# A graph layer kernel: query weights folded into the first mix weight, keys centred in their weights, one-hot rows built by ScalarE in fp32r, longer rings, and a fourth accumulator

## The reference

```
gathered = edge_vals[:, None] * xn[dst]
new_x    = segment_sum(gathered, src)            # graph branch
out1     = tanh(batchnorm(new_x @ hamilton1));   gnn = out1 @ hamilton2

q, k, v  = split(xn @ w_qkv + b_qkv)             # mix branch, 8 heads of 32
k, v     = ln(k), ln(v)                          # per head, with gain and offset
kv       = k^T v / N                             # per head, 32 x 32
ret      = q @ kv + xn
mix      = gelu(ret @ w1 + b1) @ w2 + b2 + xn

x        = x + gnn + mix
x        = x + top2_of_8_experts(layernorm(x))
```

## Time and profile before

| what | value |
|---|---|
| median of three runs | 2387.26 us |
| the profiled execution's own time | 2384.72 us |
| its span, first to last instruction | 2383.3 us |
| busy share of the span: TensorE, VectorE, ScalarE, GpSimd | 81%, 72%, 47%, 54% |
| mean granted TensorE clock | 0.89 of full speed |
| first and last put start | 108.4 and 1352.2 us |
| bytes moved by DMA, mean rate | 401.93 MB, 169 GB/s |

### The profile page before, as it was taken

One profiled execution on the slowest core, in us unless ns is written; L12 is line 12 of the kernel. 1 busy time (PEld: TensorE's weight loads), 2 busy tenths in 40 slices (PEclk: granted clock), 3 DMA queues, 4 the chain that ended last, 5 costly groups with the idle time before them and its releaser, 6 DMA issues. The chain is left out here.

```text
span 2383.3 us, 38273 instructions
## 1 busy us (share of the span) xinstructions
PE 1934.3 (81%) x11227; PEld 1607.3 (67%) x11251; DVE 1713.1 (72%) x5437; ACT 1128.4 (47%) x2236; POOL 1278.8 (54%) x811
## 2 busy tenths in 40 slices
PE   2559997697888878887877266985899999999995
PEld 1437775565665656656666134872799999999995
DVE  4848898687767858673333076888788888988884
ACT  1324443222232332323222114236899999999993
POOL 1447787578778877766777600000355444455542
PEclk8579998799998989888999598665899999999997
DMA  7878877477787787868888673223588888878885
GB/s 232 283 189 153 168 115 126 76 127 121 122 156 132 125 163 134 177 98 192 176 171 165 97 223 112 68 89 107 150 232 233 234 232 233 232 233 234 233 233 167
DMA packets 325710, 401.93 MB, mean 169 GB/s; under 512 B 34841, under 2 KB 267054, under 8 KB 325364
## 3 DMA queue, kind: packets, MB, share of 16 engines
q1 hardware_dynamic: 193822, 256.71, 34.9%
q0 software_dynamic: 103008, 103.83, 32.2%
q10 hardware_dynamic: 28662, 38.84, 5.3%
HBM read 251.12 MB, written 154.55 MB: 170 GB/s over the span
## 5 line engine op out<-in xcount | busy, mean ns | idle before, releaser
L1094 POOL DMA_INDIRECT acc_dram<-third x566 | 914.6, 1616 | 343.0 <-issue 138.6
L2016 POOL DMA_INDIRECT sum_dram<-node,small x112 | 198.2, 1770 | 316.4 <-DVE node L1945 222.7
L1873 PE MATMUL bank<-up_parts 128*128 128x256 f32 x2688 | 334.4, 284 | 2.3 <-DVE up_parts L1903 2.3
L1886 PE MATMUL bank<-down_parts 128*128 128x256 f32 x2688 | 335.4, 284 | 0.0
L1873 PEld LDWEIGHTS bank<-up_parts 128*128 128x128 f32 x2688 | 329.2, 193 | 2.7 <-DVE up_parts L1903 2.7
L1886 PEld LDWEIGHTS bank<-down_parts 128*128 128x128 f32 x2688 | 325.3, 191 | 0.0
L551 PE MATMUL bank<-work,third 128*128 128x256 f32 x1132 | 294.4, 403 | 27.8 <-ACT third L1049 27.7
L1049 ACT ACTIVATE third<-bank 128x512 f32<-128x512 f32 x283 | 168.6, 597 | 290.1 <-DMA acc_dram<-third 234.5
L857 DVE TENSOR_SCALAR third<-fixed,third 128x128 f32<-128x128 f32 x566 | 164.2, 369 | 161.0 <-PE bank L540 142.0
L1998 POOL DMA_INDIRECT node<-xh_dram,small x112 | 135.5, 1209 | 242.2 <-DVE small L1699 208.4
L551 PEld LDWEIGHTS bank<-work,third 128*128 128x128 f32 x1132 | 217.9, 205 | 63.9 <-ACT third L1049 31.6
(11 more groups left out here) (268 smaller groups left out, 3237.4 us busy)
## 6 DMA issues: line engine op xcount, KB each, us to landing
turned<-in_w_up SPq DMA_DIRECT2D x56, 1024.0 KB
turned<-in_w_down SPq DMA_DIRECT2D x56, 1024.0 KB
work<-src_dram SPq DMA_DIRECT2D x141, 256.0 KB
acc_dram<-fixed SPq DMA_DIRECT2D x15, 1280.0 KB, 13.2
work<-xn_dram SPq DMA_DIRECT2D x146, 128.0 KB
work<-acc_dram SPq DMA_DIRECT2D x72, 256.0 KB, 3.5
at_dram<-turned ACTq DMA_DIRECT2D x48, 256.0 KB
work<-at_dram ACTq DMA_DIRECT2D x24, 512.0 KB, 4.5
```

What stands on the lines that cost most here:

```text
L1094: e.indirect_dma_start(acc_dram[i], bass.IndirectOffsetOnAxis(put_i[:, t:t + 1], 0), M[:, t % (2 * QUAD), :], None, compute_op=ALU.add).th ...
L1873: k = e.matmul(ps, W1s[:, 2 * b + wp, q, h * P:(h + 1) * P], xTs[:, 2 * b + xp, q, :], start=(q == 0 and (wp, xp) == TERMS[0]), stop=(q == ...
L1886: k = e.matmul(bank[5 + c][:, 0:D], hTs[:, hp, h, c * P:(c + 1) * P], W2s[:, 2 * b + wp, h, :], start=(h == 0 and hp == 0 and wp == 0), st ...
L2016: e.indirect_dma_start(sum_dram, bass.IndirectOffsetOnAxis(slot_i[:, n:n + 1], 0), yb[:, i % 2, c, :], None, compute_op=ALU.add).then_inc( ...
```

## The change

It does these things:

1. **Folded mix weights.** Since `ret = (xn @ Wq + bq) @ KV + xn`, the product `ret @ w1` equals `xn @ (Wq KV w1 + w1)` plus a constant row. Four new key steps work out `Wq KV w1`, add it to `Wm1`, and the constant to the bias. The query product, its bias, the `KV` product and the addition of `xn` go, for all 13 chunks; 51 mix steps stay of 102.
2. **Centred key weights.** The head mean is subtracted from the columns of `Wkv` and from the bias once, so that keys and values leave TensorE centred. VectorE's sum and subtraction of each of the 49 tiles go. ScalarE squares straight from the PSUM bank, then copies.
3. **Sums beside the keys.** A column of ones stands beside the values, so that one of the two extra columns of sums comes with the 128 columns of the product.
4. **fp32r halves and ScalarE's ones.** Edge weights are split once into a high part and a rest; `one_lo` becomes two fp32r matrices, made by one `scalar_tensor_tensor` of 256 columns; `one_hi` is made on ScalarE as `relu(1 - abs(iota + far))`, two activations of 294 to 344 columns; TensorE does two fp32r matmuls. The first group's width goes from 5 to 6 (245 to 294 columns). One more step of distance lies between making and adding. `A` is set to zero by ScalarE, 512 columns at a time.
5. **Three-quad rings** for `OH` and `M`, and three buffers for the turned `A`.
6. **Four accumulators**, the fourth used from the 25th put on; 20 fills instead of 15; 100 loads instead of 75 in the node stage, and VectorE's first addition there 1024 columns wide instead of 512.
7. **Costs.** New step costs, with which the keys take quads 0 to 44, mix and dense 44 to 113, the products 113 to 137. The index is made by a maximum instead of a product and a sum.

The diff, cut to its core:

```diff
-N_ACC = 3
+N_ACC = 4
-EARLY = (4, 12)
+EARLY = (4, 12, 24)
-DENSE = ((0, 108, 5), (108, 152, 6), (152, 188, 6), (188, 216, 7))
+DENSE = ((0, 108, 6), (108, 152, 6), (152, 188, 6), (188, 216, 7))
+ROW_QUADS = 3
...
-        costs = [2.0] + [2.8] * (NT + 4) + [1.0] * 2 + cost_in_turn + [2.4] * (2 * PRODUCTS)
+        costs = [0.6] * 3 + [0.9] * NT + [0.4] * 4 + [0.5] * 4 + cost_in_turn + [0.53] * (2 * PRODUCTS)
...
         def keys_tensor(e):
-                    for i in range(2):
-                        k = e.matmul(bank[6 + g][:, P + i:P + i + 1], kvn[...i * D + g * P...], ones[0:rows, 0:1], ...)
+                    e.matmul(bank[6 + g][:, 0:P + 1], keys, beside_one, start=(t == 0), stop=False)
+                    k = e.matmul(bank[6 + g][:, P + 1:P + 2], values, ones[0:row.shape[0], 0:1], ...)
...
+            for g in range(2):
+                e.matmul(bank[6 + g][:, 0:D], KV[:, g, :], WqT[:, g, :], start=True, stop=False)
+                e.matmul(bank[6 + g][:, D:D + 1], KV[:, g, :], cols[:, 0, g:g + 1], start=False, stop=True)
+            for m in range(KC):
+                for g in range(2):
+                    k = e.matmul(bank[6 + m][:, 0:D], folded[:, g, m * P:(m + 1) * P], Wm1[:, g, :], ...)
...
         def mix_tensor(e):
-                    for q in range(KC):
-                        k = e.matmul(mix_bank(n)[:, 0:w], Wqkv[:, q, m * P:(m + 1) * P], xnT_ring[...], ...)
-                    e.matmul(mix_bank(n)[:, 0:w], KV[:, m, :], qT[:, m, 0:w], start=True, stop=True)
+                for q in range(KC):
+                    k = e.matmul(bank[5][:, 0:w], Wm1[:, q, m * P:(m + 1) * P], xnT_ring[:, c % 2, q, 0:w], ...)
...
         def dense_tensor(e):
-                for i in range(b - a + 2):
-                    t = a + i - 1
+                for i in range(b - a + 3):
+                    t = a + i - 2
+                        e.wait_ge(s_away, HOT_DONE[t])
-                        e.matmul(dense_bank(n)[:, 0:HI * s], one_lo[:, t % 4, :], one_hi[:, t % 3, 0:HI * s], ...)
+                        for i_ in range(2):
+                            k = e.matmul(dense_bank(n)[:, 0:even(HI * s)], one_lo[:, t % 4, i_, :],
+                                         one_hi[:, t % 3, 0:even(HI * s)], start=(i_ == 0), stop=(i_ == 1))
...
         def keys_vector(e):
+            centre(heads(Wkv[:, 0, :]))
+            centre(heads(Wkv[:, 1, :]))
+            centre(heads(bkv))
-                    e.tensor_reduce(ksum, rows, AX.X, ALU.add)
-                    e.scalar_tensor_tensor(out=d3, in0=spread16(ksum), scalar=-1.0 / HD, in1=rows, ...)
...
         def mix_vector(e):
-                    e.tensor_tensor(ret[:, m, 0:w], mix_bank(n)[:, 0:w], xnT_ring[:, c % 2, m, 0:w], ALU.add)
...
         def dense_vector(e):
-                        e.tensor_scalar(one_lo[:, t % 4, :], iota_p, lo_col[:, t:t + 1], w_c[:, t:t + 1], ...)
-                        e.tensor_scalar(one_hi[:, t % 3, 0:HI * s], iota_n[:, 0:HI * s], hi_col[:, t:t + 1], None, ...)
+                        e.scalar_tensor_tensor(out=one_lo[:, t % 4], in0=iota_p.unsqueeze(1).broadcast_to((P, 2, P)),
+                                               scalar=lo_col[:, t:t + 1], in1=parts_w[:, t, :]..., ...)
-                    e.memset(A, 0.0).then_inc(s_clear, 1)
...
         def keys_scalar(e):
-                    e.activation(kvq, kvn[:, t % 4, :], ACT.Square)
-                    e.activation(kvs[:, i % 2, :], bank[5][:, :], ACT.Copy)
+                    e.activation(kvq, bank[5][:, :], ACT.Square)
+                    e.activation(kvn[:, i % 5, 1:2 * D + 1], bank[5][:, :], ACT.Copy)
...
         def mix_scalar(e):
-                    e.activation(qT[:, m, 0:w], mix_bank(n)[:, 0:w], ACT.Identity, bias=cols[:, 0, m:m + 1])
...
         def dense_scalar(e):
+                        e.activation(away[:, t % 2, 0:even(HI * s)], iota_n[...], ACT.Abs, bias=far_col[:, t:t + 1])
+                        e.activation(one_hi[:, t % 3, 0:even(HI * s)], away[:, t % 2, ...], ACT.Relu, bias=ones[:, 0:1],
+                                     scale=-1.0)
+                            cleared = clear(k)
...
         def scalar_edges(e):
-                    if q >= 2:
-                        for u in (t - 2 * QUAD, t + 1 - 2 * QUAD):
+                    if q >= ROW_QUADS:
+                        for u in (t - ROW_QUADS * QUAD, t + 1 - ROW_QUADS * QUAD):
                             e.wait_ge(s_put[acc_of[u]], 16 * nth_put[u])
...
         def vector_nodes(e):
-                e.tensor_tensor(sums[:, 0, 0:n * D], sums[:, 0, 0:n * D], sums[:, 2, 0:n * D], ALU.add)
+                e.tensor_tensor(sums[:, 0:2, 0:n * D], sums[:, 0:2, 0:n * D], sums[:, 2:4, 0:n * D], ALU.add)
```

More of the change, by code:

```diff
@@ L135, in gps_layer @@
         X = node(NT, D)
+        HOT_WORDS = 4 * 2 * P + 3 * LINE
+        with nc.sbuf_tensor("hots", [P, HOT_WORDS], F32R) as hots:
+            one_lo = hots[:, 0:8 * P].rearrange("p (n a b) -> p n a b", n=4, a=2)
+            one_hi = hots[:, 8 * P:HOT_WORDS].rearrange("p (n a) -> p n a", n=3)
         turned = region("turned", NT * D)
@@ L138, in gps_layer @@
         turned.again()
+        turned(HOT_WORDS)
         A = turned(HI, P)
@@ L163, in gps_layer @@
         third = region("third", NT * D, late)
-        work = region("work", 13064, late)
+        work = region("work", 13060 + NG, late)
         src_c = third(EG * P)
         w_c = third(EG * P)
-        trash_minus = third(EG * P)
         dup = third(EG * P)
@@ L464, in mix_tensor @@
+                    if len(pair_of(c, m)):
+                        for t in pair_of(c, m):
+                            down(t)
                         yield
@@ L587, in keys_vector @@
                 vec.wait()
+                if row is b2row:
+                    for end in (0, 2 * D + 1):
+                        vec.done(e.memset(kvn[:, :, end:end + 1], 1.0))
+                    vec.wait()
                 e.scalar_tensor_tensor(out=row_b, in0=r, scalar=ident[:, 2:3], in1=row_b, op0=ALU.mult, op1=ALU.add).then_inc(s_bias, 1)
@@ L636, in keys_vector @@
                 vec.wait()
-                vec.done(e.tensor_copy(sums, bank[6 + g][:, P:P + 2]))
+                for i, at in enumerate((0 if g == 0 else P, P + 1)):
+                    vec.done(e.tensor_copy(sums[:, i:i + 1], bank[6 + g][:, at:at + 1]))
                 vec.wait()
```

448 lines of the change are left out of this document (231 added, 217 removed).

## The result

The changed kernel takes 2421.5 us (median of 4, 2417.5 to 2439.7) against 2386.1 of the kernel before on the same chip: ratio 1.0165, 95% interval 1.0109 to 1.0220. It is slower, where 2286 and faster was forecast. The profiled execution took 2417.6 us, with a span of 2416.1.

A forecast was written before the change was run, and what follows sets the result against it. GpSimd's puts were taken as the bound: minus 121 us for faster puts, plus 7 for the start, plus 13 for the read-back, minus 101 in sum, gave 2284, with the median's offset 2286 us; range 2248 to 2345.

The forecast's parts named there:

- Each engine falls below the puts' pace: Mix and dense quads: TensorE 6.2, VectorE 5.9, ScalarE 6.0 us against four puts' 7.46, so GpSimd's puts set the pace.
- the 7 us counted for the start: Start of the edge stage: five more fills delay VectorE about 20 us; 7 us taken as loss, bounds 0 and 20.
- TensorE's work: Edge stage, 147 to 1300 us: folding, centring and fp32r products cut TensorE's 964 us by 153, to 811.
- The dense products: TensorE's 216 dense tiles as fp32r pairs instead of fp32 products: 50 us saved, bounds 40 and 78.
- my partial rival: Only part of the slack is real: TensorE's clock falls, its quad takes 8.1 us, 50 us lost, 2336; chance 0.20.
- forecast 612: VectorE's edge-stage work, 147 to 1300 us: 787 us less a net 175 from dropped sums, one_hi and resets.
- ones at 0.46 us forecast: ScalarE's two activations for each of 216 dense tiles: 0.46 us each, 199 us in all, bounds 150 and 298.
- GpSimd's slow puts: Two resets that met a put held it 7.40 us, and one more like it, against 1.56: 12 us, gone.
- what the prediction left at nothing for the ones: Old one_hi and one_lo on VectorE held GpSimd's port too; their going would give some us, counted as nothing.
- The read-back: Behind the edge stage: VectorE's first addition of 25 pairs widens to 1024 columns, 0.53 us each, plus 13 us.
- The DMA rival: DMA engines become the bound of the puts: end up to 84 us later, 2370 at worst, 2330 middle; chance 0.15.
- The slower rival: ScalarE's order bounds mix and dense: quads of 11.3 us instead of 7.8, 2527, or 2406 at half; chance 0.07.

The follow-up runs named there:

- mid_after: Changed kernel with VectorE's select and indices moved between its two halves of steps, where TensorE has between and combine: 2345.7 us, ratio 0.9826.
- mid_before: Kernel before the change, with only VectorE's select and indices moved between its two halves of steps: 2369.5 us, ratio 0.9914.
- mid_costs: Changed kernel with the edits of mid_after and costs_13 together: 2312.6 us, ratio 0.9688.
- fp32_best: mid_vec_costs with one fp32 matmul for the dense product instead of two fp32r ones, and one_lo of 128 columns: 2301.7 us, ratio 0.9637.
- costs_13: Changed kernel with the planner costs of mix and dense steps times 1.3, so they take more quads with fewer steps each: 2368.3 us, ratio 0.9932.
- mid_vec_costs: mid_costs with one_hi made on VectorE instead of ScalarE: 2301.0 us, ratio 0.9655.
- ones_vector: Changed kernel with one_hi made by one VectorE comparison instead of two ScalarE activations: 2428.2 us, ratio 1.0135.
- late_after: Changed kernel with the fourth accumulator's five fills issued in quads 2 to 6 and its use starting later: 2433.7 us, ratio 1.0193.
- ones_half: Changed kernel with one_hi made by one ScalarE activation, Abs left out, so its values are wrong: 2395.1 us, ratio 1.0036.

## Why the prediction was wrong

**The step that failed** is "Each engine falls below the puts' pace". I had added the work of each engine for a mixed quad, found 6.2, 5.9 and 6.0 us, each under 7.46, and took the puts for the bound. The sums were not far off: measured over 69 quads TensorE is busy 6.9 us (473.94), VectorE 6.1, ScalarE 5.7. But three engines below 7.46 give a quad below 7.46 only if they can run apart. By theory D TensorE and VectorE can't: two dense banks tie them to one step, and VectorE's 2.9 us for the quad lay ahead of the steps, TensorE's 2.8 (652.51 to 655.29) in their middle. With a tie of one step both have to be paid. As an estimate, 2.9 + 2.8 + 3.1 tiles at about 1.1 us (additions to `A` that nothing disturbs start 0.97 and 0.87 us apart in the timeline, with mix steps between them more) is 9.1 us a quad, where 9.62 is the mean of quads 44 to 112. The runs show the direction and 76 us of it (mid_after: 9.62 to 8.57 a quad), not this sum. Its 2.8 us hold at a granted clock of 1.00; the quad before took 4.4 at 0.70. Without them it would give 6.3, and the puts' 7.46 would bound, where mid_after has 8.57. That it gives 8.7 with the 2.7 tiles of before, as measured, is luck: mid_before lays the two pieces side by side there and gained 19 us, 0.29 a quad over its 81. Nor has any run changed the tie itself, by a third dense bank. The waits in turn were on the page before (L483 idles 45.9 us for L756) and I read them as lateness of the work, not as its order.

**Where the 133 us went** (last put at 1371.4 for 1238): mix and dense 0.40 us too much for each of 283 puts, 113 us; the keys 2.01 for 1.92 and the products 2.06 for 1.93, 14 and 12; the 7 us counted for the start are to be taken off. By the runs, the order is 76 us of it (mid_after) and the division 33 more on top (mid_costs); the last 12, `one_hi` on VectorE, is inside the two intervals (0.9620 to 0.9755, 0.9610 to 0.9700). With all three the kernel takes 2301, within 15 us of the forecast and inside its range, and its last put starts at 1248.4 (1239.5 in fp32_best). That doesn't vindicate the forecast, since two of the edits are repairs and the third undoes a part of the change.

**Why slower, and not just less fast.** The division was part of the change, and I gave it no term: the new costs move mix and dense from 81 quads to 69, so that 3.1 tiles share a quad where 2.7 did. The kernel before spent 707 us on its 81 mixed quads (8.7 each), the changed one 666 on 69. What the keys won by it (367 us for 44 quads, 8.3 each; before 283 for 31, 9.1) was not enough. costs_13 bears it out: with nothing but the division edited the changed kernel is faster than the one before (0.9932). Costs that balance each engine's busy time don't balance quads with a tie in them.

**The other steps.**
- TensorE's work: forecast 811 us from 147 to 1300; the first three stretches have 905. The dense products fell by 17 us, not 50: from 147 to 1373 us L483 had 151.0 and L506 has 133.7. `between` and `combine`, unchanged, grew by 26 (167.9 and 287.0 before, 176.9 and 303.8 after) while the granted clock in mix and dense was 0.84 against 0.90, between its levels of 1.2 and 2.4 GHz. That a lower clock comes with an idler TensorE was my partial rival, and it was there. Part of it is a consequence of the waits: mid_after, with the same work for TensorE, has 0.88 (470 to 1080 us). How much of the rest is cause, no run separates; the halves themselves lower it (0.89 in mid_vec_costs, 0.96 in fp32_best). The forecast of 6.2 us a quad for TensorE, where 6.9 was measured, didn't count it.
- VectorE: forecast 612, measured 691. From 147 to 1373 us its busy time fell from 797 to 695, by 102 and not by 175. Part was my working: I took durations of groups off a busy time of stretches. Neighbouring instructions overlap in their records (L885 from 648.01 lasts 0.69, L888 starts at 648.61), and a stretch counts that once: the groups' sum fell by 141. Part were sizes: `one_lo` was sized 0.42 us and is 0.478, and the new index was counted at nothing, but L901 takes 0.268 us where its like took 0.153, 16 us over 139.
- ScalarE: ones at 0.46 us forecast, 0.53 and 0.54 measured, 33 us more over 216 tiles; that all of its work came to 581 us against 583 is therefore luck. The page "ScalarE: Activation LUTs" of the Trainium skill says, in its section on table sets, that abs and relu are in every set: the trace agrees, the edge stage after has one table load of 1.283 us at the Gelu as before. That page's rule for authors, relu and the like on VectorE, holds for the price of the work: VectorE's one comparison takes 0.407 us a tile in ones_vector, ScalarE's two activations 1.08. The kernel gained nothing by it there (1.0135 against 1.0165).
- GpSimd's slow puts: gone with the resets, the longest of 566 is 2.09 us. The rule of the Trainium skill's page "SBUF — State Buffer", section "SBUF: two separate sides", on the shared port pair agrees with that. With `one_hi` on VectorE again (ones_vector) a put takes 1.60 us in the mean, as without, so that what the prediction left at nothing for the ones shows as nothing.
- The start: 19.5 us later, forecast 20, of which I took 7 as counting; late_after shows no gain from an earlier start. The read-back: a pair's addition +0.53 us forecast, 0.51 measured. All that lies behind the last put grew by 13.6 us for the 13 forecast, but it moves by 20 us from kernel to kernel, so that this match is no proof.
- The DMA rival: not the bound in the changed kernel (0.70 in mix and dense). In mid_vec_costs the products run at a share of 1.00 with 1.93 us a put, so that case stands close behind.
- The slower rival had the right sign, and at half its price a near one (2406; a quad over 9.3 us decides, 9.66 was measured over all 69), and mostly the wrong mechanism: ScalarE's part is the 26 us of ones_half. Its chance was 0.07 because I looked for one overloaded engine.

**Open.** Whether the tie of two banks or another wait keeps mid_after at 8.57 us a quad, and how much of a mixed quad is the lower clock, is not tried. Nor is what makes mid_vec_costs take 15 us more than forecast: its quads 31 to 44 take 8.34 us, and from its last put to the end it is 1051 us, 7 more than in the changed kernel.

## What to carry to other kernels

Busy time of each engine under the budget isn't enough where two in-order engines share a double buffer: look for a pair that wait for each other in the same stretch, and lay the work that each does once an iteration at the same place of their common order. When one such engine gets less to do, read its granted clock again as well, since untouched work can get dearer by it. When costs in a planner are changed, count it as a change of its own and work out the new load of an iteration in each part. And a resource added for a bound that isn't reached yet (the fourth accumulator) shows its worth only once the earlier bound is gone, so test it again then.

## What the runs showed of the hardware

- A lone pair of fp32r matmuls of 294 columns costs TensorE 0.57 us a tile (mid_vec_costs, granted clock 0.89 in mix and dense) against 0.71 for one fp32 product of the same size (fp32_best, 0.96); 0.12 us each in a row of 48 is no price for a pair that stands alone.
- A ScalarE activation with a bias column takes 0.54 us at 294 columns, 0.58 at 344 and 0.69 at 512 (L1001, L1001, and L940 in the earlier trace rows), some 0.7 ns a column; a copy of 512 without one takes 0.60.
- VectorE's tensor_scalar on four columns took 0.268 us with a minimum and a factor from a column; the maximum of two tensors of four columns beside it, L903, 0.163.
- Fifteen fills of 1280 KB held SyncE's queue 45.0 us (ten held it 27.4), and its next load was issued only at 146.02 us.
